# A selective scan whose sums are kept by token: accumulating fp32 transposes in place of multiplications by the identity

## What is computed

```python
xz = jnp.einsum('bld,ed->ble', x, W_in)
u, z = jnp.split(xz, 2, axis=-1)
u_c = silu(causal_conv(u) + conv_b)
dt_r, Bm, Cm = jnp.split(u_c @ W_x.T, [8, 24], axis=-1)
dt = softplus(dt_r @ W_dt.T + b_dt)
A = -exp(A_log)
# over time, per channel and state n:
#   h = exp(dt * A[n]) * h + (dt * u_c) * B[n];   y += h * C[n]
y = y + u_c * D
y = y * silu(z)
out = y @ W_out.T
```

## Time and profile before

| | before |
|---|---|
| median of 3 runs | 570.88 us (568.62 to 573.11) |
| span of the profiled execution | 569.1 us |
| PE busy in the span | 468.3 us (82%) |
| DVE busy | 416.4 us (73%) |
| ACT busy | 316.7 us (56%) |
| POOL busy | 318.1 us (56%) |
| chain that ended last | PE 32%, DVE 26%, issue 17%, ACT 11%, POOL 9%, DMA 4% |

### The profile page before, as it was taken

How to read it: one execution, slowest core, us unless ns; L and a number is a source line. 1 busy time by engine, 2 the same in 40 slices (tenths; PEclk the granted TensorE clock), 3 DMA queues, 4 the chain that set the end, 5 groups by cost and what they waited for, 6 DMA issues and landing times.

```text
span 569.1 us, 7422 instructions
## 1 busy us (share of the span) xinstructions
PE 468.3 (82%) x2101; PEld 267.8 (47%) x2102; DVE 416.4 (73%) x832; ACT 316.7 (56%) x656; POOL 318.1 (56%) x298
## 2 busy tenths in 40 slices
PE   0994778797978999899797997878787875889996
PEld 0742455465636985363232433223332331459973
DVE  4278968587256426499999799999999899563333
ACT  2664365465262644567675976787656852345521
POOL 1029743253554215347779678899889876432155
PEclk9997898799679999989998999999888989998999
DMA  8999940000004431255564456456543561023423
GB/s 292 418 327 332 311 136 1 1 2 20 18 29 121 117 102 40 63 158 144 156 149 130 134 156 139 151 126 184 155 135 130 160 148 37 21 64 109 122 70 93
DMA packets 39993, 73.96 MB, mean 130 GB/s; under 512 B 4368, under 2 KB 20240, under 8 KB 39184
## 3 DMA queue, kind: packets, MB, share of 16 engines
q1 hardware_dynamic: 35024, 66.74, 39.5%
q0 software_dynamic: 2048, 4.20, 2.7%
q10 hardware_dynamic: 2880, 2.55, 1.4%
HBM read 66.00 MB, written 26.28 MB: 162 GB/s over the span
## 4 chain that ended last, share of the span: by engine, by line
PE 32%; DVE 26%; issue 17%; ACT 11%; POOL 9%; DMA 4%; SPq 1%; ACTq 0%; DVEq 0%; POOLq 0%
DVE arena L1298 10%; PE psum L732 5%; PE psum L680 5%; POOL arena L1880 4%; DVE psum L1292 3%; PE psum L862 3%; PE psum L744 2%; POOL arena L1834 2%; PE psum L693 2%; PE psum L781 2%; ACT L1376 2%; ACT xn L1406 2%; ACT arena L1688 1%; POOL by_expert L1797 1%; PE psum L717 1%
## 5 line engine op out<-in xcount | busy, mean ns | idle before, releaser
L1880 POOL TENSOR_TENSOR arena<-arena 128x512 f32<-128x512 f32 x127 | 158.1, 1269 | 50.8 <-DVE arena L1298 50.5
L862 PE MATMUL psum<-arena,w 128*128 128x512 f32 x256 | 135.9, 644 | 29.9 <-POOL arena L1880 27.3
L1298 DVE TENSOR_TENSOR_SCAN arena<-arena,psum 128x512 f32<-128x512 f32 x128 | 148.4, 1200 | 7.8 <-ACT arena L1688 4.2
L1688 ACT ACTIVATE arena<-arena 128x510 f32<-128x510 f32 x128 | 87.2, 713 | 42.3 <-DVE arena L1298 39.9
L862 PEld LDWEIGHTS psum<-arena,w 128*128 128x128 f32 x256 | 45.3, 199 | 105.8 <-POOL arena L1880 81.6
L1292 DVE TENSOR_TENSOR psum<-psum,arena 128x512 f32<-128x512 f32 x128 | 81.4, 681 | 0.7 <-DMA arena<-bc_store 0.7
L680 PE MATMUL psum<-xnt,w 128*128 128x512 f32 x128 | 62.4, 636 | 0.0
L1765 POOL TENSOR_TENSOR arena<-arena 128x512 f32<-128x512 f32 x16 | 20.3, 1267 | 74.9 <-DVE arena L997 74.9
L1834 POOL DMA_INDIRECT arena<-by_expert,routes x32 | 30.9, 965 | 35.4 <-DMA by_expert<-arena 20.0
L1797 POOL DMA_INDIRECT by_expert<-xn,routes x32 | 31.9, 995 | 14.5 <-issue 7.7
L1163 DVE TENSOR_TENSOR arena<-psum,arena 128x512 f32<-128x512 f32 x24 | 16.5, 690 | 30.8 <-PE psum L680 22.0
(11 more groups left out here) (198 smaller groups left out, 817.5 us busy)
## 6 DMA issues: line engine op xcount, KB each, us to landing
arena<-bc_store SPq DMA_DIRECT2D x64, 512.0 KB, 4.8
by_expert<-w_in SPq DMA_DIRECT2D x4, 4096.0 KB, 43.4
w<-w_in SPq DMA_DIRECT2D x1, 4427.5 KB, 13.0
arena<-by_expert SPq DMA_DIRECT2D x54, 64.0 KB, 1.9
by_expert<-arena SPq DMA_DIRECT2D x52, 64.0 KB, 1.6
by_expert<-w_in SPq DMA_DIRECT2D x1, 1984.0 KB, 66.9
x<-x_in SPq DMA_DIRECT2D x4, 256.0 KB, 7.4
out<-x SPq DMA_DIRECT2D x4, 256.0 KB, 2.3
```

The source lines that it names most:

```text
L862: nc.tensor.matmul(bank(6 + c), ident, state[c][s % 3], start=False, stop=(n == DS - 1)).then_inc(*summed.inc((s, c)))
L1298: nc.vector.tensor_tensor_scan(state[c][s % 3], decay_b[c][s % 2], bank(2 + c), 0.0, ALU.mult, ALU.add).then_inc(*state_ready.inc((s, c)))
L1688: nc.scalar.activation(live, seq, ACT.Exp, scale=a_neg[:, DS * c + n:DS * c + n + 1]).then_inc(*decay_ready.inc((s, c)))
L1880: nc.gpsimd.tensor_tensor(state[c][s % 3], state[c][s % 3], bc_row[s % len(bc_row)][:, 1, :], ALU.mult).then_inc(*y_done.inc((s, c)))
```

## The change

For the groups g = 0, 1, 2 the sums are kept by token: 128 tokens in the partitions, 256 channels in the columns, two blocks of tokens in bank 6 and two in bank 7.

- add_up makes of each 128 x 512 state four transposes of 128 x 128 (matmul with is_transpose against ident, the state as weights), which accumulate in PSUM. The term u * D of a step n = 0 is eight products of 128 x 128 ahead of both halves. Summed is released by the last transpose of a half.
- z of these groups is projected by token too (two products of 256 columns for a bank instead of one of 512) and kept flat in z_cols. Silu and the two gates work on the same numbers of elements as before; gate 0 and 1 now take the first and second two blocks.
- The gated block is by token, while the projection wants channels in the partitions. So a new step "turn gated" (lateness 3, PE) transposes it back, 2 x 4 transposes into two banks of end_ring, and a new step "take gated" (lateness 4, ACT) copies them to dtu, 2 copies of 128 x 512. project_out goes from lateness 4 to 5 and reads dtu; "add" stays at 5.
- "sums" now waits for both halves at once. The last group is left as it was.

```diff
@@ -245,7 +245,11 @@
-u, z, dt_b, dtu = (piece(NCH * NTOK).rearrange("p (c t) -> p c t", c=NCH) for _ in range(4))
+u = piece(NCH * NTOK).rearrange("p (c t) -> p c t", c=NCH)
+z_cols = piece(NCH * NTOK)
+z = z_cols.rearrange("p (j d) -> p j d", j=NBLK)
+z_last = z_cols[:, NCH * BANK * (NGRP - 1):].rearrange("p (c t) -> p c t", c=NCH)
+dt_b, dtu = (piece(NCH * NTOK).rearrange("p (c t) -> p c t", c=NCH) for _ in range(2))
@@ -305,7 +309,7 @@
 def due_in_steps(s):
...
-    what = {0: ["sums"], 1: ["gate 0"], 2: ["gate 1"], 4: ["project_out"], 5: ["add"], 6: ["squares"], 7: ["root"], 8: ["turn"], 9: ["logits"],
+    what = {0: ["sums"], 1: ["gate 0"], 2: ["gate 1"], 3: ["turn gated"], 4: ["take gated"], 5: ["project_out", "add"], 6: ["squares"], 7: ["root"], 8: ["turn"], 9: ["logits"],
@@ -415,8 +419,10 @@
-past_ready, gated_b = signal("past_ready", [0]), signal("gated_b", chan_events[:-NCH])
-sums_taken = signal("sums_taken", chan_events[:-NCH])
+half_events = [(g, h) for g in GROUPS[:-1] for h in range(2)]
+past_ready, gated_b = signal("past_ready", [0]), signal("gated_b", half_events)
+sums_taken = signal("sums_taken", half_events)
+gated_turned, gated_taken = signal("gated_turned", chan_events[:-NCH]), signal("gated_taken", chan_events[:-NCH])
@@ -795,11 +801,17 @@
 def project_z(g, c, ring):
...
-    nc.tensor.matmul(b, in_b[:, DI + P * c:DI + P * c + P], xnt_group(g), start=True, stop=True).then_inc(*zb_projected.inc((g, c)))
+    if g == NGRP - 1:
+        r = nc.tensor.matmul(b, in_b[:, DI + P * c:DI + P * c + P], xnt_group(g), start=True, stop=True)
+    else:
+        for q, j in enumerate(blocks(g)[2 * c:2 * c + 2]):
+            r = nc.tensor.matmul(b[:, DI * q:DI * q + DI], xnt_block(j), in_b[:, DI:2 * DI], start=True, stop=True)
+    r.then_inc(*zb_projected.inc((g, c)))
@@ -851,15 +863,51 @@
     elif what == "turn":
...
+def by_token(q, c):
+    at = DI * (q % 2) + P * c
+    return bank(6 + q // 2)[:, at:at + P]
 def add_up(s):
+    g, n = steps[s]
+    if g == NGRP - 1:
+        return add_up_last(s)
+    if n == 0:
+        pe.wait_ge(*(u_ready[g] if g else past_ready[0]))
+        for q, j in enumerate(blocks(g)):
+            if q % 2 == 0:
+                pe.wait_ge(*(sums_taken[g - 1, q // 2] if g else shared_added[0, NGRP - 1]))
+            for c in range(NCH):
+                nc.tensor.matmul(by_token(q, c), u[:, c, P * j:P * j + P], past[:, c, :],
+                                 start=(q % 2 == 0 and c == 0), stop=False, skip_group_check=True)
+    for c in range(NCH):
+        pe.wait_ge(*y_done[s, c])
+        for q in range(GB):
+            r = nc.tensor.matmul(by_token(q, c), state[c][s % 3][:, P * q:P * q + P], ident, start=False, stop=(n == DS - 1),
+                                 is_transpose=True, skip_group_check=True)
+        r.then_inc(*summed.inc((s, c)))
+def add_up_last(s):
...
-            pe.wait_ge(*(sums_taken[g - 1, c] if g else shared_added[0, NGRP - 1]))
-            pe.wait_ge(*(u_ready[g] if g else past_ready[0]))
+            pe.wait_ge(*sums_taken[g - 1, c])
+            pe.wait_ge(*u_ready[g])
...
+def turn_gated(g, ring):
+    for c in range(NCH):
+        b, free = ring.take(gated_taken[g, c])
+        scan_bank["gated", g, c] = b
+        for f in free:
+            pe.wait_ge(*f)
+        for q, j in enumerate(blocks(g)):
+            pe.wait_ge(*gated_b[g, q // 2])
+            r = nc.tensor.transpose(b[:, P * q:P * q + P], z[:, j, P * c:P * c + P], ident)
+        r.then_inc(*gated_turned.inc((g, c)))
@@ -867,20 +915,23 @@
-    pe.wait_ge(*(gated_b[g, c] if g < NGRP - 1 else gated_last[c]))
+    pe.wait_ge(*(gated_taken[g, c] if g < NGRP - 1 else gated_last[c]))
...
+gated = dtu[:, :, group(g)] if inner else z_last
...
-        r = nc.tensor.matmul(b[:, P * q:P * q + P], z[:, c, P * j:P * j + P], wt("out_b")[:, DM * c:DM * c + DM],
+        r = nc.tensor.matmul(b[:, P * q:P * q + P], gated[:, c, P * q:P * q + P], wt("out_b")[:, DM * c:DM * c + DM],
...
 for what, g in due_in_steps(s):
-    if what == "project_out":
+    if what == "turn gated":
+        turn_gated(g, end_ring)
+    elif what == "project_out":
@@ -1303,7 +1354,7 @@
-nc.vector.tensor_tensor(z[:, c, group(g)], bank(6 + c), z[:, c, group(g)], ALU.mult).then_inc(*gated_last.inc(c))
+nc.vector.tensor_tensor(z_last[:, c, :], bank(6 + c), z_last[:, c, :], ALU.mult).then_inc(*gated_last.inc(c))
@@ -1592,7 +1643,8 @@
 def take_z(g, c):
...
-    nc.scalar.activation(z[:, c, group(g)], scan_bank["z", g, c], ACT.Copy).then_inc(*zb_taken.inc((g, c)))
+    at = NCH * BANK * g + BANK * c
+    nc.scalar.activation(z_cols[:, at:at + BANK], scan_bank["z", g, c], ACT.Copy).then_inc(*zb_taken.inc((g, c)))
@@ -1674,7 +1726,8 @@
 elif what == "silu gate":
...
-    nc.scalar.activation(z[:, :, group(g)], z[:, :, group(g)], ACT.Silu).then_inc(*zb_ready.inc(g))
+    gate_cols = z_cols[:, NCH * BANK * g:NCH * BANK * (g + 1)]
+    nc.scalar.activation(gate_cols, gate_cols, ACT.Silu).then_inc(*zb_ready.inc(g))
@@ -1697,9 +1750,13 @@
 for what, g in due_in_steps(s):
     if what == "sums":
+        act.wait_ge(*summed[DS * (g + 1) - 1, NCH - 1])
+        for h in range(2):
+            nc.scalar.activation(dtu[:, h, group(g)], bank(6 + h), ACT.Copy).then_inc(*sums_taken.inc((g, h)))
+    elif what == "take gated":
...
-            act.wait_ge(*summed[DS * (g + 1) - 1, c])
-            nc.scalar.activation(dtu[:, c, group(g)], bank(6 + c), ACT.Copy).then_inc(*sums_taken.inc((g, c)))
+            act.wait_ge(*gated_turned[g, c])
+            nc.scalar.activation(dtu[:, c, group(g)], scan_bank["gated", g, c], ACT.Copy).then_inc(*gated_taken.inc((g, c)))
@@ -1884,10 +1941,12 @@
 for what, g in due_in_steps(s):
     if what in ("gate 0", "gate 1"):
-        c = ("gate 0", "gate 1").index(what)
+        h = ("gate 0", "gate 1").index(what)
+        at = NCH * BANK * g + BANK * h
...
-        pool.wait_ge(*sums_taken[g, c])
-        nc.gpsimd.tensor_tensor(z[:, c, group(g)], dtu[:, c, group(g)], z[:, c, group(g)], ALU.mult).then_inc(*gated_b.inc((g, c)))
+        pool.wait_ge(*sums_taken[g, h])
+        nc.gpsimd.tensor_tensor(z_cols[:, at:at + BANK], dtu[:, h, group(g)], z_cols[:, at:at + BANK],
+                                ALU.mult).then_inc(*gated_b.inc((g, h)))
```

## The result

| | before | after |
|---|---|---|
| median of 6 runs each, taken together | 569.96 us (568.34 to 573.11) | 577.75 us (576.85 to 578.3) |
| ratio, 95% interval | | 1.0149 (1.0112 to 1.0187) |
| span of the profiled execution | 569.1 us | 576.8 us |
| PE busy in the span | 468.3 us | 454.6 us |
| DVE busy | 416.4 us | 416.6 us |

A forecast was written before the change was run, and what follows sets the result against it. The prediction took DVE to bound the scan, so that only DVE's idle time could change. Its terms, -1.3 - 0.8 + 1.1 + 1.5 = +0.5 us, put on the median of 570.88, gave 571.4 us, range 567 to 576.5.

The forecast's parts named there:

- The transposes' price: In add_up on PE: a 128 x 128 transpose costs 0.11 us at full clock, 0.22 at 0.50, accumulating ones the same.
- PE down by 30 to 40 us: Sign of being right: PE's busy time falls by 30 to 40 us, from cheaper sums in 48 steps.
- Step 19: DVE's 4.2 us stall for ACT's decay shrinks as PE's sums and taps end sooner: -1.3 us, bounds 0 and -2.5.
- Step 53: Stall behind a late z product shrinks as step 49's sums get cheaper on PE: -0.8 us, bounds 0 and -1.7.
- The walk through group 1 at full clock: Group 1's closing, gate 1 to root: the longer chain makes the root late, +1.1 us of DVE idle.
- Groups 0 and 2 cost 0: Their closings: root 0.6 us later, hidden by slack, with 0.4 and 0.7 us left in hand.
- The clock: Closings of three groups: lighter PE gets 0.50, about half a hit each, less slack: +1.5 us, bounds 0 and 5.
- Rival 2: Steps with transposes alone leave PE at 0.50, so every closing starts there: 577.6 us, chance 0.13.
- Rivals 1 and 3: First: stalls at steps 19 and 53 go entirely, 563.5 us, chance 0.07; third: nothing happens, 569.5 us, chance 0.25.
- The range: Whole kernel's time: own range from the terms' bounds taken half together, 568.5 to 574 us; whole range 567 to 576.5.
- What would show it: Signs: step 19 wait about 3 us, group 1 root wait 1 to 3, "add" waiting for PE, more stretches at 0.50.

The follow-up runs named there:

- fill: Changed kernel with three extra fp32 products of 512 columns on PE ahead of turn gated's wait for the gates; 574.43 us, ratio 1.0046.
- products: Changed kernel with the sums by token made by ordinary fp32 products in place of transposes, order and waits the same; 577.5 us, ratio 1.011.
- turn_behind: Changed kernel with turn gated issued behind the sums of the same step instead of ahead of them; 575.33 us, ratio 1.0092.
- warm_out: Changed kernel plus zero products in the first 48 steps, except in closing chains and step 15, and two products ahead of the gate wait; 570.05 us, ratio 0.9997.
- clock: Kernel before with 400 transposes, 100 products, 200 transposes ahead of all PE work; transposes 0.110 us apart from 12.8 us on; no total time given.
- half: Kernel before with sums of the last 256 of 512 columns left out in groups 0 to 2, except each last step; 570.15 us, ratio 0.9996.
- warm_dt: As warm_out, with group 3's second dt moved from step 36 to 38 on PE and 37 to 39 on ACT; 572.25 us, ratio 1.0027.

## Why the prediction was wrong, step by step

- *The transposes' price* was right: 0.11 us each at 1.00 and 0.22 at 0.50, accumulating or not. "PE down by 30 to 40 us" was not met (468.3 to 454.6, 13.7 us): the work halved, but much of it, and of all else on PE, ran at half the clock.
- *Step 19*, forecast -1.3: measured -1.45, by the steps given. That it came so close is in part luck: by where the low clock fell, the same code took 6.12 to 7.06 us in other profiles, where this one has 6.26.
- *Step 53*, forecast -0.8: measured +0.95. This step of the sum was an error in reading the change. The sums of step 49 belong to group 3, the last, which the change leaves as it was; in the profile after they are still products, four records, and then the z product, all at 0.50:

```profile
442.43 3.78 PE L898 MATMUL psum<-arena,w 128*128 128x512 f32 x4 [3.38 <-POOL arena L1937]
446.00 1.92 PE L810 MATMUL psum<-xnt,w 128*128 128x512 f32 x2
```

  In the earlier trace rows the same four took 3.68; the z product behind them took 1.02 there, at full clock, and 1.92 here. Nothing was removed. The 0.9 is the clock's in this one profile, and not the change's: `fill`, `products` and `turn_behind`, with the same code there, took 6.82 to 6.92 us for the step.
- *The walk through group 1 at full clock*, forecast +1.1: right in its steps (gate to "add" 6.5 us, forecast 6.44; "add" to the root 6.03, forecast 6.04). `warm_out` runs the same chain at full clock, and its steps 38 to 41 are 1.23 us longer than before. But only 0.60 of that is the wait for the root that the walk named; the rest is the centre that lasts as long as POOL's products, which the forecast did not have. The number agrees partly by luck.
- *Groups 0 and 2 cost 0*: group 2 yes; group 0 not in after, where DVE's centre waits 3.05 us. At full clock it was right: in `fill` group 0 costs nothing and the root is 0.29 us early, where the forecast had 0.4 in hand. In `warm_out` a product of zeros (0.86 us) stands ahead of the second dt, ACT waits 0.43 us for that dt between "add" and squares, the root is 0.20 us late, and with the long centre that costs 1.24 us. With 0.29 us in hand, a delay of half a microsecond cost more than twice its length.
- *The clock*, forecast +1.5, bounds 0 and 5: **the step that failed**. Measured by `warm_out` against after it is 7.1 us in the profiles, 7.7 us by the medians of the runs, and 8.7 us by their ratios. The working took "half a hit" of one stretch of 3.4 us, as in the earlier trace rows, for each closing. In its place came 10 us at 0.50 in the closings of group 0 and group 1 each, over the whole chain, so that "add" started 11.06 us behind the gate and not 6.44. One stretch of before was taken for the size of all of them, though there PE filled the stretch with taps and products of 512 columns, and here the idle wait for the gate (4.63 us in group 0, 2.82 in group 1) stands between light steps. The low clock also hits twice in group 1: "add" late makes the decays behind it late (steps 39, 40), and then the root.
- *Rival 2* (577.6) came within 0.2 us of the time, and its mechanism is the nearest. That the number fits is luck: its terms are not what was measured, group 0 +2.1 against +3.7, group 1 +3.6 against +5.6, group 2 +1.8 against 0, step 19 0 against -1.45, step 53 -0.8 against +0.95. And its condition, that transposes by themselves leave PE at 0.50, fell with `clock` and `half`: the clock was at 0.83 in the stage, and products of the same amount had the same.
- *Rivals 1 and 3* are out: no stall went entirely, and the root was not in time.
- *The range*: half of the bounds given, below the forecast (1.2, 0.9 and 1.5 us), leads to 569.6, not to the 568.5 that stands there. It changes nothing here.
- *What would show it*: the wait at step 19, the new wait of the centre, "add" waiting in all three groups (8.2 us in three) and more stretches at 0.50 were all there. Of the wait for the root the forecast allowed 1 to 3 us in group 1: 1.89; it did not have the one in group 0, nor the wait for the decay between.

Group 2 was spared for a reason that fits this. Its closing runs beside the steps of group 3, whose sums are still products. Timeline of PE after, in that closing:

```profile
451.69 3.60 PE L898 MATMUL psum<-arena,w 128*128 128x512 f32 x8
455.90 1.10 PE L922 MATMUL psum<-x,w 128*128 128x512 f32 x2 [0.61 <-ACT arena L1759]
456.83 1.95 PE L925 MATMUL psum<-w,arena 128*128 128x128 f32 x16
```

All of it is at full clock, as project_out was before, and steps 54 to 58 are as long as before. The heavy neighbour is there, and the clock with it. This was read from the trace and not tried by itself.

What stays open: that a centre which misses the end of the scan lasts as long as POOL's products was seen four times and not tried; why the ratios give `warm_out` 1 us more over after than the medians do; how far the single profiles stand for the runs, given how steps 19 and 53 vary; and whether a version with the new chain can be had that is faster than before; the two that tried, `warm_out` and `warm_dt`, reached 0.9997 and 1.0027.

## What to carry to other kernels

Work that lies beside the bound is not free to remove: ask where the clock goes when it is gone, and which chain of that engine has less slack than its own length at full clock. A new dependent chain and a lighter engine should be priced together, at 1.00 and at 0.50, and not each by itself. Slack that a walk leaves in hand should be compared with what the next delay would cost, which here was 1.24 us for a root that was late by 0.20. And before a term is booked at a place, see there which branch of the new code runs: the stall at step 53 stood in the one group that the change leaves out.
